# Finishing y ahead of the statistics of t on VectorE, and clipping y first on GpSimd

## The reference, cut to what matters

```python
x = x + conv_ref(ln_c(x), ...)     # per quadrant and head: 16 centers, cosine, argmax, weighted sum
t = to_tokens(x)
t = t + ffn_ref(ln_t(t), W1, b1, W2, b2)

# inside ffn_ref, for each group g of 6 images (5 groups; the last 2 images get zero):
y = einsum(h, sign(W2)) + b2
gamma = max(abs(y[g]))                      # over the whole group
out[g] = clip(y * 128 / (gamma + EPS), -128 + EPS, 128 - EPS)
```

## Time and profile before

| | us |
|---|---|
| median of 3 runs | 3002.28 |
| the profiled execution's own time | 3013.11 |
| its span, first to last instruction | 3011.3 |

### The profile page before, as it was taken

One profiled execution on the slowest core, in us unless ns is written; L12 is line 12 of the kernel. 1 busy time (PEld: TensorE's weight loads), 2 busy tenths in 40 slices (PEclk: granted clock), 3 DMA queues, 4 the chain that ended last, 5 costly groups with the idle time before them and its releaser, 6 DMA issues.

```text
span 3011.3 us, 62497 instructions
## 1 busy us (share of the span) xinstructions
PE 2836.4 (94%) x20998; PEld 1931.7 (64%) x20998; DVE 2695.2 (90%) x6308; ACT 2246.1 (75%) x4894; POOL 1561.1 (52%) x2739
## 2 busy tenths in 40 slices
PE   3999999999999999999999999999999999999987
PEld 2666666656666666666666556666665666666555
DVE  3689989899999989999999999999989999998976
ACT  2577777897777779777777987777779777777963
POOL 1344444575555543455555665555543555554854
PEclk9899999999999999999999999999999999999989
DMA  1011111002222210122222002222210222221025
GB/s 45 17 34 34 33 41 34 9 17 66 66 65 66 65 49 1 49 65 66 66 65 58 25 17 65 65 71 73 69 33 3 72 72 66 66 65 50 1 73 153
DMA packets 30930, 154.27 MB, mean 51 GB/s; under 512 B 6483, under 2 KB 6804, under 8 KB 30612
## 3 DMA queue, kind: packets, MB, share of 16 engines
q1 hardware_dynamic: 30612, 150.28, 18.0%
HBM read 75.60 MB, written 74.66 MB: 50 GB/s over the span
## 4 chain that ended last, share of the span: by engine, by line
PE 68%; ACT 15%; POOL 6%; issue 6%; DVE 5%; SPq 0%; DMA 0%; POOLq 0%; DVEq 0%; ACTq 0%
PE ps L963 20%; PE ps L1040 10%; ACT nT L457 9%; PE ps L1023 6%; PE ps L971 6%; PE ps L900 5%; PE ps L911 4%; ACT turns L560 4%; POOL turns L433 4%; PE ps L1096 3%; PE ps L919 3%; PE ps L1033 2%; DVE turns L838 2%; PE ps L1013 2%; PE ps L987 2%
## 5 line engine op out<-in xcount | busy, mean ns | idle before, releaser
L488 ACT ACTIVATE sq<-ps 112x384 f32<-112x384 f32 x896 | 444.8, 497 | 562.5 <-PE ps L963 547.6
L963 PE MATMUL ps<-wfT,xn 97*112 97x384 f32 x1792 | 736.4, 509 | 3.1 <-ACT sq L488 3.1
L1040 PE MATMUL ps<-tok,w1T 98*128 98x392 f16 x2880 | 617.9, 330 | 8.9 <-ACT turns L563 8.7
L396 POOL TENSOR_TENSOR csq<-cbd 96x128 f32<-96x128 f32 x128 | 50.6, 396 | 803.9 <-DVE cbd L662 803.9
L433 POOL CAST turns<-turns 128x392 f16<-128x392 f32 x240 | 319.8, 1346 | 205.1 <-ACT turns L560 201.1
L678 DVE TENSOR_REDUCE n<-sq 112x32 f32<-112x1536 f32 (+1 forms) x256 | 395.2, 1544 | 22.5 <-ACT sq L488 22.3
L1040 PEld LDWEIGHTS ps<-tok,w1T 98*128 98x128 f16 x2880 | 277.2, 100 | 182.9 <-issue 52.9
L769 DVE TENSOR_REDUCE hmax<-ps 128x1 f32<-128x392 f32 x720 | 380.8, 556 | 3.4
L457 ACT ACTIVATE xnT<-ps,mo_x 112x96 f32<-112x96 f32 x896 | 302.8, 442 | 98.1 <-POOL mo_x L388 98.1
L838 DVE SCALAR_TENSOR_TENSOR turns<-turns 128x1176 f16<-128x1176 f32 x240 | 331.0, 1379 | 0.0
L560 ACT ACTIVATE turns<-ps,scale 128x1176 f32<-128x1176 f32 x240 | 323.2, 1346 | 2.2 <-DVE scale L792 1.1
(11 more groups left out here) (140 smaller groups left out, 5859.9 us busy)
## 6 DMA issues: line engine op xcount, KB each, us to landing
xbuf<-in_x SPq DMA_DIRECT2D x64, 588.0 KB, 4.8
out<-xbuf SPq DMA_DIRECT2D x64, 588.0 KB, 6.0
turns<-out SPq DMA_DIRECT2D x60, 588.0 KB, 6.4
out<-turns SPq DMA_DIRECT2D x60, 588.0 KB, 4.4
tok<-in_L_ffn_W SPq DMA_DIRECT2D x2, 142.5 KB
cst<-in_constants SPq DMA_DIRECT2D x1, 195.0 KB
wf<-in_L_conv_Wf SPq DMA_DIRECT2D x1, 144.0 KB
tok<-in_L_conv_Wv SPq DMA_DIRECT2D x1, 144.0 KB
```

The costliest lines, as they stand in the source:

```text
L488: nc.scalar.activation(sq[:, t, :], bank(2 + t % 2, TN, D), ACT.Square).then_inc(f_sq, 1)
L963: mm(bank(2 + t % 2, TN, D), xn[:, k % 2, t * TN:(t + 1) * TN], wfT[:, :], start=True, stop=True)\
L1040: ins = mm(dst, w1T[:, c * 128:(c + 1) * 128], tok[:, bass.ds(place, 1), part, s * HT:(s + 1) * HT].rearrange("p a n -> p (a n)"), start=p ...
```

## The change

In the first pass of the groups that have FINAL steps, for every place but 0:

- VectorE's `finish` goes from behind the second norms to the place in front of the statistics of t, behind `center_floor`.
- GpSimd's `clipped` goes from behind `center_norms` to the head of the slot's list.

At place 0, and in the last part, both stay where they were. For all groups GpSimd's `center_squares` goes from the end of slot j (for the quadrant 4 ahead) to the head of slot j+1 (lag 1, the same quadrant), behind the early clip. No instruction is added or removed, and no wait is new.

```diff
+        def ahead_of_tokens(part, place):
+            return part != "last" and place > 0
...
-            def clipped(g, part):
+            def clipped(g, part, early):
                 def step(k, q, place, use):
+                    if early != ahead_of_tokens(part, place):
+                        return
...
             def attention(g, part):
-                return [(A, 0, marks), (X, 1, center_norms), (R, 0, clipped(g, part), FINAL),
-                        (R, 0, moments("t", EPS_T), FFN), (X, 0, moments("x", EPS_C)), (X, 0, center_squares)]
+                return [(R, 0, clipped(g, part, True), FINAL), (X, 1, center_squares), (A, 0, marks), (X, 1, center_norms),
+                        (R, 0, clipped(g, part, False), FINAL), (R, 0, moments("t", EPS_T), FFN),
+                        (X, 0, moments("x", EPS_C))]
...
-            def finish(part):
+            def finish(part, early):
...
                 def step(k, q, place, use):
+                    if early != ahead_of_tokens(part, place):
+                        return
+                    if part != "last":
+                        one(k, q, place, use)
+                        return
                     for d in in_tail(place):
                         one(d % BODY, GROUPS * GQ + d, d, GROUPS * BODIES + d // BODY)
-                return step if part == "last" else one
+                return step
...
-                        (A, 1, residual(1)), (X, 1, center_floor), (R, 0, stats("t", 6, g), FFN), (M, 0, norms(0, TA)),
-                        (A, 0, masked), (X, 0, stats("x", 0)), (M, 0, norms(TA, T)), (R, 0, finish(part), FINAL),
+                        (A, 1, residual(1)), (X, 1, center_floor), (R, 0, finish(part, True), FINAL), (R, 0, stats("t", 6, g), FFN),
+                        (M, 0, norms(0, TA)), (A, 0, masked), (X, 0, stats("x", 0)), (M, 0, norms(TA, T)),
+                        (R, 0, finish(part, False), FINAL),
```

## The result

The changed kernel takes 2985.41 us (median of 4 runs, 2980.01 to 2986.55) where the kernel before takes 3002.23: 0.9935 of it, 95% interval 0.9917 to 0.9954. On a second chip it is 2982.74 against 3009.31 us: 0.9918, 0.9901 to 0.9935. So the medians are 0.6 and 0.8% lower, 17 and 27 us. The forecast was 3036 us, slower; the time is nearest to that of rival (a), 2981 us.

The account below looks back on a forecast made before the run. TensorE's chain was taken as the bound. Slots would go from 18.38 us to 18.15 without the finish's hold, plus 0.60 for the clip's stop: 92 x 0.37 = 34 us more, 3002.3 to 3036 us, range 2977 to 3054.

Parts of the forecast that it names:

- rival (a): Short VectorE steps are not stopped by the early clip, or it waits for them: slot 18.15 us, 2981 us; chance 0.27.
- What bounds the kernel: TensorE's chain; in middle-group slots the finish delays GpSimd's moments of x, making ScalarE and TensorE wait: 0.23 us a slot.
- The finish leaving its old place: GpSimd's line 384 takes 0.21 us again and ScalarE's wait goes: 92 x 0.23 = 21 us less.
- Moving `center_squares`: On GpSimd, it waits for the same cbd as before and starts marks at the same time: cost 0.
- The finish in its new place: It fits VectorE's 0.92 us wait behind `center_floor` with 0.05 us left; cinv is held but in time: cost 0.
- The clip in its new place: Beside VectorE's inverse root it stops line 702 or 704 until it ends, about 0.85 us; ends 0 and 0.9 us.
- What a stop would cost: n_low(1) comes late and TensorE's tile 1 waits: 0.60 us a slot, 18.75 us instead of 18.15.
- rival (b): The clip stops line 709 alone, VectorE 0.3 to 0.6 us late: slot 18.15 to 18.5, about 2996 us; chance 0.13.
- The chances: The forecast 0.60, (a) 0.27, (b) 0.13; faster 0.31, same 0.09, slower 0.60.

Follow-up runs that it names:

- e7: Kernel before, finish of places 1 to 23 of the middle groups replaced in its old place by a one-input reduction: 2980.1 us, ratio 0.9905.
- e9: Changed kernel with three unread matmuls ahead of the fifth half quadrant of each second pass: 2989.2 us, ratio 0.9945 to the kernel before.
- e10: Kernel before with three unread matmuls ahead of the fifth half quadrant of each second pass: 3011.0 us, ratio 1.0017.
- e5: Changed kernel with an extra y*scale+t into a scratch tile ahead of each early finish on VectorE: 3060.7 us, slot 18.85 us.
- e15: Changed kernel with one reduction of 100 constants on VectorE ahead of line 707 in groups 1 to 4: 3043.7 us, one run.
- e11: Changed kernel with two reductions of constants, about 0.86 us together, on VectorE ahead of line 707 in groups 1 to 4: 3045.3 us.
- e2: Changed kernel with the clip back in its old place in GpSimd's list, working a slot ahead: 2984.3 us, ratio 0.9921 to the kernel before.
- e13: Changed kernel with one reduction of two constants on VectorE ahead of line 707 in groups 1 to 4: 2980.7 us, one run.

## Why the prediction was wrong

- **What bounds the kernel** was read rightly. The 0.23 us of a slot were the finish shutting GpSimd out at line 384 (e7: 18.15 us with the place in VectorE's list unchanged).
- **The finish leaving its old place**, 21 us less: right. Measured 22.0 us within the groups, 21.8 us between e9 and e10. Moving `center_squares` cost nothing, as forecast: the first group has that move too and keeps its 18.15 us.
- **The finish in its new place**, cost nothing: right, to hundredths. It starts at 892.56, the statistics of t follow without a wait, cinv is held until 894.00 and is in time, eq keeps its 1.71 us. e5 shows how full the place is:

```diff
+                    if early:
+                        v.scalar_tensor_tensor(scratch[:, :], y_of(place), scale[0:C, 1:2], t, ALU.mult, ALU.add)
                     v.scalar_tensor_tensor(t, y_of(place), scale[0:C, 1:2], t, ALU.mult, ALU.add).then_inc(S["final"], 1)
```

> The changed kernel with an extra y*scale+t into a scratch tile ahead of each early finish: VectorE is busy there 0.94 us longer. It measures how much room is left in front of the statistics of t. By the trace the finish ends just as TensorE's turned t is there, so none: the slot should grow by 0.8 to 0.95 us, to about 19.0 us, and the span by 75 to 85 us. If VectorE had slack elsewhere in the loop the slot would grow by less.

The slot grew by 0.70 us, so of a second finish's 0.94 us a quarter found room elsewhere in the loop, more than I had expected.
- **The clip in its new place**: this is the step that failed. "So the ends are 0 (short steps slip past) and 0.9 us (line 702 or 704 stands until the clip ends). I take the upper end": the lower end came. The clip starts at 902.29, line 708 at 902.35, and the rows that I rested on did not answer which of two that start 0.06 us apart wins. In the earlier trace rows the GpSimd cast was 0.26 us ahead of VectorE's. I read its outcome as a rule for any lead, though I had put the lead at 0.04 us myself. The runs put the limit between 0.15 and 0.24 us: up to 0.15 us such steps pass, between 0.16 and 0.20 us both happen, and from 0.24 us on they stand. Of line 704 the forecast was wrong in this kernel for the same reason: its counterpart starts 0.18 us behind the clip and keeps its 0.18 us. That it can be stopped at all, which the forecast took for granted, is right: in nine slots of e15 it stands 0.82 or 0.83 us, from 0.29 us behind the clip on.
- **What a stop would cost**, 0.60 us a slot: right. e11 has 0.67 for a delay made by other means, e15 has 0.59 with the very collision, and TensorE's wait stands where the forecast put it.
- **Rival (a)** gave the time (2981 us against 2985 and 2983), and **rival (b)** the picture: line 709 alone is stopped. It costs nothing (e2). (b) had sized the stop at 0.3 to 0.6 us; it is 0.23.
- **The chances** were the second error. A case whose sign hangs on some hundredths of a microsecond, as the text itself said of (b), did not deserve 0.60 on one side. Which side came was luck of the edit: with 0.16 us more work on VectorE ahead of line 707 (e15) the slot is 18.74 us, the forecast's 18.75.

The Trainium skill, page "SBUF — State Buffer", section "Who interferes with whom", has it that the instruction that issues first keeps the port pair for its whole length. For line 708 that gave the wrong winner if the shown starts are taken for the order of issue: the clip's shown start is first, and VectorE's step went ahead. For leads of 0.24 us and more the traces agree with the page (e15, 0.84 us instead of 0.21); between 0.16 and 0.20 us nine steps pass and 169 stand.

## What to carry to other kernels

A VectorE instruction with two SBUF inputs can cost more than its own time, as 0.23 us a slot here: ask what GpSimd has to do meanwhile, and put it where GpSimd can wait; replacing it by one of equal length with one input (e7) tells in one run what its hold on GpSimd is worth. When two engines are to meet within 0.1 or 0.2 us of each other, a prediction can only say that it may go either way; the change may hold or collapse with the next edit that shifts one of them, as a reduction of 100 constants did here (e15: 18.74 us a slot and 3044 us). And before two kernels are compared to a few tenths of a per cent, look whether some other stage has two patterns that a small delay switches.

## What the runs showed of the hardware that was not expected

- Whether a GpSimd clip of 0.99 us stops a short VectorE step goes by some hundredths of a microsecond. With two SBUF inputs the step passes if its shown start is up to 0.15 us behind the clip's, either may happen from 0.16 to 0.20 us, and it stands from 0.24 us on. With one SBUF input it passed up to 0.25 us and stood at 0.29 to 0.33 us (e15). What passes lengthens the clip: 1.02 to 1.07 us in most slots of the changed kernel and e15, 1.12 to 1.14 in e13, 0.99 with none.
- A GpSimd power is not like the clip: in the trace of before, line 697, with two SBUF inputs, starts inside it in over 120 slots and keeps its 0.22 us, and the power, but for one, its 1.48 to 1.50.
- A one-column power on GpSimd that starts 0.16 us behind a finish takes 1.28 us instead of 0.55. It ends 0.42 us behind the finish, which fits a hold at its start; the trace shows no more than its start and end.
- The second pass has two steady patterns, 2.07 and 2.18 us per half quadrant on average, with the same instructions. Which one a pass falls into is settled near its start: every pass with a stretch of TensorE's lower clock (0.50, 1.2 GHz) there was short and every one without was long, in 70 passes, and added matmuls ahead of the fifth half quadrant make it short without such a stretch (e10). Why TensorE's clock drops at the starts of some passes and not of others was not tried and stays open.
